# Four of sixteen block transfers issued by ScalarE's queue, and a new order at the end of layer 2

## Chip, cores and metric

The kernel runs on one core of one Trainium2 chip. The metric is device time in microseconds (us), the median of the runs; lower is better.

## The reference

Sixteen independent graphs of 1024 nodes with 64 features pass through four graph-attention layers, each followed by a residual and a layer norm. All four are masked by the same adjacency matrix. Layer 2, at whose loop and end most of the change stands, has eight heads:

```python
def _L2_gnn_ref(atom_embeddings, edges, Wq, bq, Wk, bk, Wv, bv, edge_bias, Wp, bp):
    ...
    scores = jnp.einsum('bmhd,bnhd->bhmn', q, k) * scale
    scores = scores + jnp.transpose(edge_bias[edges], (0, 3, 1, 2))
    scores = jax.nn.leaky_relu(scores, NEG_SLOPE)
    scores = jnp.where(mask, scores, jnp.asarray(-1000000000.0, dtype=scores.dtype))
    attn = jax.nn.softmax(scores, axis=-1)
    out = jnp.einsum('bhmn,bnhd->bmhd', attn, v).reshape(b, m, h * d)
    return out @ Wp + bp
```

Layer 3 scores a pair of nodes by 64 products behind a leaky ReLU:

```python
    s = u[:, :, None, :] + v[:, None, :, :]
    s = jnp.where(s > 0, s, ALPHA * s)
    e = jnp.einsum('bijf,f->bij', s, a[:, 0])
```

## The kernel before, in words

All order is written by hand: each engine has one program, and semaphores tie them together. The programs loop over the graphs. In one turn of the loop an engine does layer 3 of graph g, with layers 0 and 1 of graph g+1 woven into it (`ahead`), and then layer 2 of graph g+1.

**Layer 2** works on 64 tiles of 128 rows by 1024 columns: four pairs of heads, eight row blocks each, two heads. Tiles 2s and 2s+1 are step s (32 steps). One tile passes through:

- TensorE `scores` (L665, L669): mask, then q times x in two parts, into one of two PSUM slots, `score[n % 2]`. It waits until VectorE has read tile n-2 of that slot (`s_leaky`).
- ScalarE `relu` (L944), the first pass, PSUM to `probs[n % 4]`. From tile 4 on it waits until tile n-4 has been turned (`s_blocks`).
- VectorE `leaky` (L1243): adds the score, and finds the least of each row.
- ScalarE `exps` (L951): the exponential, with row sums.
- VectorE `turn_tile`: `dve.transpose` (L1271) turns each 32x32 block within the tile and writes it to `blocks[k % 2]`.

Four tiles (two steps) make a group or quad k. To turn the whole matrix, the 32x32 blocks must still change partitions. That is done by transfers: `move` (L380) on SP's queue issues sixteen, each from 32 partitions to 32 others, 128 KB, into `quadT[k % 3]`. Quads 0 to 14 are moved (`MOVED`). Quad 15 isn't: TensorE turns its four tiles against the identity (L522), and VectorE copies them out of PSUM (L1276) into `blocks[1]`, for which it waits until quad 13 has been moved out of it. VectorE waits for the transfers of quad k-2 before it writes quad k, TensorE for those of quad k before the products.

TensorE `pv_quad` (L697) multiplies the turned quad by the values `vw` in two halves, each 16 matmuls. It is called at step s with quad s//2 - LAG, half s % 2, from s = 2*LAG = 6 on. After the four quads of a pair, ScalarE copies the sums out (`copy_out`, L959, half at t = 2 and half at t = 6 of the next pair), TensorE turns them (`turn_heads`, L522), VectorE divides by the row sums (`pair_out`, L1284), and GpSimd adds. `extra_use` says at which step of a pair q and `vw` of the next pair are made, and heads are turned. For the next graph SP loads eight adjacency tiles between the groups (`next_adj`, L367) and GpSimd converts them out of `adj_in` (L1438 to L1443).

At the end of the program's layer 2 stand the last step, the remaining halves of quads 12 and 13, quads 14 and 15, and the heads of pair 3.

**Start of layer 3**: VectorE adds the last heads (L1364) and normalizes; x2 (L1188) is turned by TensorE. TensorE does first the first products of the next graph (L527, L544) and `KEEP` = 24 matmuls whose result isn't used (L776). From x2 follow v3 and ucol (L1021, L1022 on ScalarE, one half of the partitions each), and with them the 128 groups of the layer: ScalarE (L1035) and VectorE (L1379) make operands, TensorE multiplies (L808). `move` also carries layers 0, 1 (64 KB each) and 3 (32 KB each).

The lines that the change touches most are these:

```python
for turn_ in range(4):
    for a in range(4):
        c = (a + turn_) % 4
        sp.dma_start(dst[32 * c:32 * c + 32, :, a, :], src[32 * a:32 * a + 32, :, c, :]).then_inc(done, 16)
```

## Time and profile before

| | |
|---|---|
| median of 3 runs | 9054.23 us (9046.0 to 9068.25) |
| the profiled execution | 9052.68 us |
| its span, first to last instruction | 9050.9 us |
| mean granted TensorE clock | 0.958 of full speed |
| TensorE, VectorE, ScalarE, GpSimd busy | 90%, 82%, 78%, 16% |
| DMA: the dynamic queue q1 | 810.76 MB, 40.9% of 16 engines' time |

The profile is of one execution. "Busy" is the share of the span in which an engine runs an instruction; issuing transfers doesn't count as busy. "SPq" is the queue of SP. The chain of waits follows the last instruction back to what released it, and so on to the start; its shares tell which engine or queue the end of the program hung on. One graph takes some 553 us: layer 2 about 195, its end and the start of layer 3 some 45, and layer 3 the rest.

### The profile page before, as it was taken

The numbers are of one execution on the slowest core, as the hardware profiler recorded it, in microseconds if no ns is written. First come the engines' busy times: TensorE is split into PE (matmuls) and PEld (weight loads), VectorE is DVE, ScalarE is ACT, GpSimd is POOL, SyncE is SP. The second block draws the span as 40 slices with busy tenths as digits, with TensorE's granted clock in tenths as the row PEclk, the third lists the DMA queues.
The fourth block names the chain that finished last, engine by engine and source line by source line (L and its number), as shares of the span: only waits on it lengthen the run. The fifth ranks groups of instructions, "written<-read, shape, count | busy, mean of one in ns | idle before, by whom it ended". The sixth has DMA issues, their size and how long they took to land.

```text
span 9050.9 us, 165102 instructions
## 1 busy us (share of the span) xinstructions
PE 8158.5 (90%) x57976; PEld 3621.5 (40%) x57976; DVE 7394.6 (82%) x11173; ACT 7034.4 (78%) x8220; POOL 1429.1 (16%) x582
## 2 busy tenths in 40 slices
PE   3899998989999899998998989899898998999999
PEld 1434435343353433434334353443534435343352
DVE  3788787987879878798787978878788787987878
ACT  2788786977869778787787878778688786977877
POOL 0301203021030301203012030120302103021000
PEclk7999999999999999999999999999999999999999
DMA  2715426253362623527145271542715426253251
GB/s 72 159 35 114 101 50 155 42 129 80 66 139 50 144 58 78 129 46 165 37 100 112 47 167 35 114 98 53 155 39 120 91 49 155 44 132 75 56 126 19
DMA packets 2150347, 822.58 MB, mean 91 GB/s; under 512 B 1146914, under 2 KB 2129954, under 8 KB 2147362
## 3 DMA queue, kind: packets, MB, share of 16 engines
q1 hardware_dynamic: 2149410, 810.76, 40.9%
q8 instruction: 507, 8.31, 0.4%
q14 instruction: 430, 3.52, 0.1%
HBM read 76.25 MB, written 4.19 MB: 9 GB/s over the span
## 4 chain that ended last, share of the span: by engine, by line
PE 36%; SPq 21%; DVE 18%; issue 13%; ACT 8%; DMA 3%; DVEq 0%; POOL 0%; ACTq 0%; POOLq 0%
SPq L380 20%; PE psum L808 19%; DVE work L1379 6%; ACT work L1035 5%; PE psum L527 3%; PE psum L697 3%; DVE work L1271 3%; DVE work L1243 3%; PE psum L599 2%; PE psum L522 2%; PE psum L544 1%; PE psum L776 1%; DMA work<-work 1%; PE psum L669 1%; ACT spare L877 1%
## 5 line engine op out<-in xcount | busy, mean ns | idle before, releaser
L808 PE MATMUL psum<-work,pick 128*32 128x512 f32 x32768 | 3758.0, 598 | 198.1 <-DVE work L1379 162.2
L1035 ACT ACTIVATE work<-spare,ucol 128x1024 f32<-128x1024 f32 x3402 | 3633.7, 1147 | 52.0 <-PE psum L808 48.6
L1379 DVE TENSOR_SCALAR work<-spare,ucol 128x1024 f32<-128x1024 f32 x4790 | 3250.2, 745 | 305.8 <-ACT ucol L1022 233.7
L808 PEld LDWEIGHTS psum<-work,pick 128*32 128x32 f32 x32768 | 975.9, 110 | 2532.0 <-issue 2065.5
L944 ACT ACTIVATE work<-psum,beta 128x1024 f32<-128x1024 f32 x1024 | 1138.9, 1112 | 474.0 <-PE psum L669 395.6
L1271 DVE STREAM_TRANSPOSE work<-work 128x1024 f32<-128x1024 f32 x960 | 1191.1, 1241 | 295.3 <-DMA work<-work 177.1
L1243 DVE CUSTOM_DVE_ANT_0 work<-psum,work 128x1024 f32<-128x1024 f32 x1024 | 1225.7, 1197 | 155.0 <-ACT work L944 143.6
L951 ACT ACTIVATE work<-work,least 128x1024 f32<-128x1024 f32 x1024 | 1172.2, 1145 | 54.7 <-DVE least L1243 54.5
L665 PE MATMUL psum<-mask,ident_b 128*128 128x512 bf16 x2048 | 643.5, 397 | 304.3 <-DVE least L1243 301.0
L1460 POOL TENSOR_TENSOR rstd<-rstd,neg_half 128x8 f32<-128x8 f32 x64 | 131.6, 2056 | 4951.5 <-DVE rstd L1182 4951.5
L669 PE MATMUL psum<-x_split,q_hi 128*128 128x512 f32 x2048 | 862.0, 503 | 0.0
L697 PE MATMUL psum<-work,vw 128*64 128x256 f32 x5632 | 701.7, 393 | 0.0
L669 PE MATMUL psum<-x_split,q_lo 128*128 128x512 f32 x2048 | 660.2, 404 | 0.0
L1438 POOL TENSOR_SCALAR mask_next<-adj_in 128x1024 bf16<-128x1024 int32 x120 | 436.4, 3637 | 442.8 <-DMA adj_in<-in_adj 434.7
L697 PEld LDWEIGHTS psum<-work,vw 128*64 128x64 f32 x5632 | 384.4, 140 | 285.6 <-issue 130.2
L669 PEld LDWEIGHTS psum<-x_split,q_hi 128*128 128x128 f32 x2048 | 405.1, 198 | 159.9 <-issue 15.5
L1440 POOL TENSOR_SCALAR no_edge<-adj_in 128x1024 bf16<-128x1024 int32 x120 | 436.1, 3634 | 9.5
L669 PEld LDWEIGHTS psum<-x_split,q_lo 128*128 128x128 f32 x2048 | 398.1, 194 | 92.3
L1146 DVE CUSTOM_DVE_ANT_0 spare<-psum,spare 128x1024 f32<-128x1024 f32 x256 | 311.2, 1216 | 110.5 <-ACT spare L872 107.3
L665 PEld LDWEIGHTS psum<-mask,ident_b 128*128 128x128 bf16 x2048 | 125.2, 99 | 688.3 <-DVE least L1243 524.0
L872 ACT ACTIVATE spare<-psum,sbias 128x1024 f32<-128x1024 f32 x256 | 284.4, 1111 | 91.2 <-PE psum L582 77.9
L599 PE MATMUL psum<-q_lo,vw 128*64 128x256 f32 x2048 | 262.9, 401 | 67.3 <-DMA q_lo<-spare 37.1
(161 smaller groups left out, 6985.1 us busy)
## 6 DMA issues: line engine op xcount, KB each, us to landing
work<-work SPq DMA_DIRECT2D x2560, 128.0 KB, 2.5
spare<-work SPq DMA_DIRECT2D x1280, 128.0 KB, 2.5
adj_in<-in_adj SPq DMA_DIRECT2D x128, 512.0 KB, 4.9
q_lo<-adj_in SPq DMA_DIRECT2D x1024, 64.0 KB, 2.1
q_lo<-spare SPq DMA_DIRECT2D x1024, 64.0 KB, 2.1
work<-work SPq DMA_DIRECT2D x1792, 32.0 KB, 1.9
mask<-mask_next SPq DMA_DIRECT2D x16, 2048.0 KB, 9.3
x_in<-in_x SPq DMA_DIRECT2D x16, 256.0 KB, 9.6
```

What stands on the lines that cost most here:

```text
L380: sp.dma_start(dst[32 * c:32 * c + 32, :, a, :], src[32 * a:32 * a + 32, :, c, :]).then_inc(done, 16)
L599: mm = pe.matmul(dst, values[layer][:, j, :], src[:, j, :, :, :], start=(j < 2), stop=(j >= NT - 2))
L665: pe.matmul(slot[:, cols], ident_b[:], mask[:, t, cols], start=True, stop=False)
L669: mm = pe.matmul(slot[:, cols], left, x_split[:, cols], start=False, stop=(k == 1))
L697: mm = pe.matmul(dst, vw[:, pair % 2, j, F * h:F * h + F], src[:, j, :, h, :].rearrange("p a (t i) -> p a t i", t=2), start=(j == 0), stop ...
L808: mm = pe.matmul(slot[32 * q:32 * q + 32, cols], pick[:, 15 - kk:47 - kk], ring[kk % 4][q][:, cols], start=False, stop=(kk == 15), skip_gr ...
L944: act.activation(probs[n % 4], score[n % 2], ACT.Relu, bias=beta4[:, t, 2 * pair + h:2 * pair + h + 1], scale=GAIN[2]).then_inc(s_relu, 1)
L951: act.activation(probs[n % 4], probs[n % 4], ACT.Exp, bias=least[:, n % 4:n % 4 + 1], scale=-1.0, accum_out=rowsum[:, pair % 2, 2 * t + h: ...
L1035: ins = act.activation(ring[kk % 4][q], v3, ACT.Relu, bias=ucol[:, 4 * T + q, kk:kk + 1])
L1243: dve.tensor_tensor_reduce(probs[n % 4], score[n % 2], probs[n % 4], -ALPHA[2], 3.0e38, ALU.add, ALU.min, least[:, n % 4:n % 4 + 1]).then_ ...
L1271: dve.transpose(dst[:, :, h, half, :], probs[n % 4].rearrange("p (b j) -> p b j", j=32))\
L1379: ins = dve.tensor_scalar(ring[kk % 4][q], v3, ucol[:, 4 * T + q, kk:kk + 1], 0.0, ALU.add, ALU.max)
```

## The change

- SP's `move` gets a number of turns. For a quad of layer 2 it does three (twelve transfers). The fourth (four transfers) is issued by ScalarE in the new `move_quad`, called in its even steps s = 2, 4, ... 30 for quad s//2 - 1, after `relu` of tile 2s+2 and before `exps` of tile 2s+1. It waits for the fourth transpose of the quad, and, as SP does, for the buffers. Both count on the same semaphore.
- `LAG` is 5 and counts steps: `pv_quad` is called from s = 5 on, one step earlier than before. The heads, `vw` and the two `copy_out` of a pair come one step earlier too.
- The unmoved tiles 60 to 63 are copied to `last_rows`: tiles 60 and 61 to `adj_in`, free once GpSimd has converted the next adjacency, and tiles 62 and 63 to `work[4:6]`, free after quad 12. Their products are two halves by row block (`pv_last`), sixteen matmuls of 128 columns each. Step 31 is taken out of the loop and written out.
- The last `pair_out` moves from VectorE's layer 2 to the start of its layer 3, behind the loop's branch. `column_low` goes behind x2. The upper half of ucol is made by VectorE, not ScalarE.
- `KEEP` is 16.

```diff
-LAG = 3
+LAG = 5
-KEEP = 24
+KEEP = 16
...
-            def move(dst, src, done):
-                for turn_ in range(4):
+            def move(dst, src, done, turns=4):
+                for turn_ in range(turns):
...
-                    move(dst, src, s_moved[k % 4])
+                    move(dst, src, s_moved[k % 4], 3)
...
+            def pv_last(it, half):
+
+                in_sbuf(pe, it, ("tile", TILES2 - 3 + 2 * half))
+                src = last_rows[half].rearrange("p (b a h i) -> p b a h i", a=4, h=2, i=32)
+                cols = slice((NT - 2 + half) * P, (NT - 1 + half) * P)
+                for j in range(NT):
+                    for h in range(2):
+                        mm = pe.matmul(outT[F * h:F * h + F, cols], vw[:, (HP - 1) % 2, j, F * h:F * h + F],
+                                       src[:, j, :, h, :], start=(j == 0), stop=(j == NT - 1))
...
-                    if s >= 2 * LAG:
-                        pv_quad(g, it, s // 2 - LAG, s % 2, tail)
+                    if s >= LAG:
+                        pv_quad(g, it, (s - LAG) // 2, (s - LAG) % 2, tail)
...
-                pv_quad(g, it, QUADS - 3, 1, tail)
-                for k in (QUADS - 2, QUADS - 1):
-                    pv_quad(g, it, k, 0, tail)
-                    pv_quad(g, it, k, 1, tail)
+                pv_quad(g, it, MOVED - 2, 0, tail)
+                turn_tile(g, it, TILES2 - 2)
+                pv_quad(g, it, MOVED - 2, 1, tail)
+                turn_tile(g, it, TILES2 - 1)
+                pv_last(it, 0)
+                pv_quad(g, it, MOVED - 1, 0, tail)
+                pv_quad(g, it, MOVED - 1, 1, tail)
+                pv_last(it, 1)
...
+            def move_quad(g, k, tail):
+
+                act.wait_ge(s_blocks, g * 4 * MOVED + 4 * k + 4)
+                if k >= 3:
+                    act.wait_ge(s_pv, g * QUADS + k - 2)
...
+                src = blocks[k % 2].rearrange("p (b c x) -> p b c x", c=4, x=P)
+                dst = quadT[k % 3].rearrange("p (b c x) -> p b c x", c=4, x=P)
+                for a in range(4):
+                    c = (a + 3) % 4
+                    act.dma_start(dst[32 * c:32 * c + 32, :, a, :], src[32 * a:32 * a + 32, :, c, :])\
+                       .then_inc(s_moved[k % 4], 16)
...
                     exps(g, n)
                     if more:
                         relu(g, n + 2)
+                    if s and s % 2 == 0:
+                        move_quad(g, s // 2 - 1, tail)
...
+                if h == 0 and half == 0:
+                    dve.wait_ge(s_mask_next, g + 2)
+                if h == 0 and half == 1:
+                    dve.wait_ge(s_pv, g * QUADS + MOVED - 2)
```

ScalarE's instructions in layer 2 of the first graph, from step 2's first exponential on. Before (L951 is the exponential, L944 the first pass, L899 the copy of a q):

```order
L951 ACTIVATE work,rowsum<-work,least 128x1024 [waits s_leaky]
L944 ACTIVATE work<-psum,beta 128x1024 [waits s_scores,s_blocks]
L951 ACTIVATE work,rowsum<-work,least 128x1024 [waits s_leaky]
L944 ACTIVATE work<-psum,beta 128x1024 [waits s_scores,s_blocks]
L951 ACTIVATE work,rowsum<-work,least 128x1024 [waits s_leaky]
L944 ACTIVATE work<-psum,beta 128x1024 [waits s_scores,s_blocks]
L899 ACTIVATE q_hi<-psum 128x1024 [waits s_turned]
L951 ACTIVATE work,rowsum<-work,least 128x1024 [waits s_leaky]
```

After (the same passes are now L960, L953 and L908):

```order
L960 ACTIVATE work,rowsum<-work,least 128x1024 [waits s_leaky]
L953 ACTIVATE work<-psum,beta 128x1024 [waits s_scores,s_blocks]
L985 DMA work<-work 32x8x128 [waits s_blocks]
L985 DMA work<-work 32x8x128 x3
L960 ACTIVATE work,rowsum<-work,least 128x1024 [waits s_leaky]
L953 ACTIVATE work<-psum,beta 128x1024 [waits s_scores,s_blocks]
L960 ACTIVATE work,rowsum<-work,least 128x1024 [waits s_leaky]
L953 ACTIVATE work<-psum,beta 128x1024 [waits s_scores,s_blocks]
L908 ACTIVATE q_hi<-psum 128x1024 [waits s_turned]
```

The four transfers with their wait now stand between a first pass and the next exponential; this comes fifteen times in a layer.

TensorE's end of layer 2, from the last scores on (L522 turns a tile of `work` or the heads, L697 are products, eight rows to a head and half). Before:

```order
L522 MATMUL psum<-ident,work 128x128 [waits s_probs,s_turn_free]
L522 MATMUL psum<-ident,work 128x128 x7
L522 MATMUL psum<-ident,heads_T 128x128 [waits s_copied,s_turn_free]
L522 MATMUL psum<-ident,heads_T 128x128 x7
L697 MATMUL psum<-work,vw 64x4x2x32 x8
L522 MATMUL psum<-ident,work 128x128 [waits s_probs,s_turn_free]
L522 MATMUL psum<-ident,work 128x128 x7
L697 MATMUL psum<-work,vw 64x4x2x32 [waits s_quad_moved1]
L697 MATMUL psum<-work,vw 64x4x2x32 x7
L522 MATMUL psum<-ident,work 128x128 [waits s_probs,s_turn_free]
L522 MATMUL psum<-ident,work 128x128 x7
L697 MATMUL psum<-work,vw 64x4x2x32 x8
```

After (L523 turns, L695 are products of moved quads, L708 those of the unmoved tiles):

```order
L523 MATMUL psum<-ident,work 128x128 [waits s_probs,s_turn_free]
L523 MATMUL psum<-ident,work 128x128 x7
L695 MATMUL psum<-work,vw 64x4x2x32 [waits s_quad_moved1]
L695 MATMUL psum<-work,vw 64x4x2x32 x7
L523 MATMUL psum<-ident,work 128x128 [waits s_probs,s_turn_free]
L523 MATMUL psum<-ident,work 128x128 x7
L695 MATMUL psum<-work,vw 64x4x2x32 x8
L523 MATMUL psum<-ident,work 128x128 [waits s_probs,s_turn_free]
L523 MATMUL psum<-ident,work 128x128 x7
L708 MATMUL psum<-adj_in,vw 64x128 [waits s_turn_free]
L708 MATMUL psum<-adj_in,vw 64x128 x15
L695 MATMUL psum<-spare,vw 64x4x2x32 [waits s_quad_moved2,s_copied]
```

The turn of pair 2's heads and the second half of quad 12 have gone to an earlier step, and between the last tile's turn and quad 14 stand the products of tiles 60 and 61. Before, quads 14 and 15 followed whole; after, quad 14 and then sixteen L708 for tiles 62 and 63.

## Rows read from the trace of the kernel before

**Rows 1.** The page: busy time by engine, and the chain by line.

```profile
PE 8158.5 (90%) x57976; PEld 3621.5 (40%) x57976; DVE 7394.6 (82%) x11173; ACT 7034.4 (78%) x8220; POOL 1429.1 (16%) x582
...
SPq L380 20%; PE psum L808 19%; DVE work L1379 6%; ACT work L1035 5%; PE psum L527 3%; PE psum L697 3%; DVE work L1271 3%; DVE work L1243 3%; PE psum L599 2%; PE psum L522 2%; PE psum L544 1%; PE psum L776 1%; DMA work<-work 1%; PE psum L669 1%; ACT spare L877 1%
```

**Rows 2.** Timeline of SP's queue, ninth graph: start us, length us, instructions xcount.

```profile
4710.99 11.10 SPq L380 DMA_DIRECT2D spare<-work  x16
...
4722.42 0.36 SPq L367 DMA_DIRECT2D adj_in<-in_adj  x1
...
4759.41 23.14 SPq L380 DMA_DIRECT2D work<-work  x32
```

**Rows 3.** The line L380: duration ns min/median/max.

```profile
L380 SPq DMA_DIRECT2D work<-work x4352: 585/613/2072, 278.9 to 9018.4; - x198
...
L380 SPq DMA_DIRECT2D q_lo<-adj_in x1024: 585/611/1702, 64.5 to 8477.3; - x171
```

**Rows 4.** Timeline of ScalarE, start of layer 2; in brackets: [idle before <-releaser].

```profile
4665.45 1.12 ACT L944 ACTIVATE work<-psum,beta 128x1024 f32<-128x1024 f32 x1
...
4668.10 1.11 ACT L944 ACTIVATE work<-psum,beta 128x1024 f32<-128x1024 f32 x1 [1.53 <-PE psum L669]
...
4674.98 1.12 ACT L944 ACTIVATE work<-psum,beta 128x1024 f32<-128x1024 f32 x1
...
4679.24 1.13 ACT L944 ACTIVATE work<-psum,beta 128x1024 f32<-128x1024 f32 x1
...
4689.51 1.02 ACT L899 ACTIVATE q_hi<-psum 128x1024 fp32r<-128x1024 f32 x1 [4.73 <-PE psum L527]
```

**Rows 5.** ScalarE by line, whole layer 2 (busy, mean ns | idle before); its last exponential.

```profile
L951 ACT ACTIVATE work<-work,least 128x1024 f32<-128x1024 f32 x64 | 73.3, 1145 | 4.3 <-DVE least L1243 4.3
...
L944 ACT ACTIVATE work<-psum,beta 128x1024 f32<-128x1024 f32 x64 | 71.2, 1113 | 29.7 <-PE psum L669 23.5 <-DVE work L1271 6.0
...
L903 ACT ACTIVATE vw<-psum 128x1024 f32<-128x1024 f32 x3 | 3.1, 1027 | 1.6 <-PE psum L564 1.6
...
4859.10 1.15 ACT L951 ACTIVATE work<-work,least 128x1024 f32<-128x1024 f32 x1 [0.87 <-DVE least L1243]
```

**Rows 6.** Timeline of TensorE and VectorE, steps 17 and 18 of layer 2.

```profile
4771.77 1.19 DVE L1243 CUSTOM_DVE_ANT_0 work<-psum,work 128x1024 f32<-128x1024 f32 x1
...
4771.81 0.61 PE L665 MATMUL psum<-mask,ident_b 128*128 128x512 bf16 x2
...
4772.88 1.24 DVE L1271 STREAM_TRANSPOSE work<-work 128x1024 f32<-128x1024 f32 x1
...
4776.51 0.60 PE L665 MATMUL psum<-mask,ident_b 128*128 128x512 bf16 x2
```

**Rows 7.** Timeline of all engines, end of layer 2; then one TensorE group by line.

```profile
4843.64 2.12 POOL L1443 TENSOR_TENSOR mask_next<-mask_next,no_edge 128x1024 bf16<-128x1024 bf16 x1
...
4856.70 1.23 DVE L1276 COPY work<-psum 128x1024 f32<-128x1024 f32 x1 [2.53 <-DMA work<-work]
...
4871.61 3.62 PE L697 MATMUL psum<-spare,vw 128*64 128x256 f32 x32
...
4880.52 1.22 DVE L1284 TENSOR_TENSOR heads_T<-psum,rinv 128x1024 f32<-128x1024 f32 x1 [9.19 <-PE psum L522]
...
L762 PE MATMUL psum<-work,vw 128*64 128x128 f32 x16 | 1.1, 279 | 0.0
```

**Rows 8.** Timeline of all engines, start of layer 3.

```profile
4889.74 0.76 DVE L1188 TENSOR_TENSOR x<-zb,rstd 128x256 f32<-128x256 f32 x2
...
4890.63 6.55 PE L776 MATMUL psum<-mask,ident_b 128*128 128x512 bf16 x24
...
4906.50 0.60 PE L801 MATMUL psum<-mask,ident_b 128*128 128x512 bf16 x2
```

**Rows 9.** Windows: PE, PEld, DVE, ACT, POOL busy; clock, DMA share, GB/s.

```profile
4735.00:4758.00 23.00, 20.87 (x120) 12.30 (x120) 20.63 (x26) 18.64 (x26) 2.46 (x2) 1.00 0.95 212
...
4761.00:4783.00 22.00, 19.40 (x118) 11.42 (x117) 19.93 (x26) 17.62 (x25) 15.06 (x6) 1.00 0.80 181
```

More of the change, by code:

```diff
@@ L64, in extra_use @@
     pair, t = divmod(s, NT)
-    if t == 7 and pair:
+    if t == 6 and pair:
         return ("heads", pair - 1)
     if pair + 1 < HP:
-        return {3: ("q", 2 * pair + 2), 4: ("q", 2 * pair + 3), 6: ("vw", pair + 1)}.get(t)
+        return {3: ("q", 2 * pair + 2), 4: ("q", 2 * pair + 3), 5: ("vw", pair + 1)}.get(t)
     return None
@@ L230, in build @@
         quadT = [quad_of(4), quad_of(16), spare[:]]
-        def turned_quad(k):
-            return quadT[k % 3] if k < MOVED else blocks[k % 2]
+        last_rows = [adj_in[:].rearrange("p a b -> p (a b)").bitcast(F32),
+                     work[:, 4:6, :].rearrange("p a b -> p (a b)")]
         probs3 = [work[:, 6 + i, :] for i in range(2)]
@@ L712, in layer2 @@
                 scores(g, it, 1, tail)
-                for s in range(STEPS2):
-                    pair, t = divmod(s, NT)
+                for s in range(STEPS2 - 1):
                     n = 2 * s
-                    more = s + 1 < STEPS2
                     extra = extra_use(s)
-                    if more:
-                        scores(g, it, n + 2, tail)
+                    scores(g, it, n + 2, tail)
                     if extra:
@@ L985, in layer2 @@
                         elu3(tail)
-                    if t == 2 and pair:
+                    if t == 1 and pair:
                         copy_out(g, pair - 1, 0)
-                    if t == 6 and pair:
+                    if t == 5 and pair:
                         copy_out(g, pair - 1, 1)
@@ L1264, in turn_tile @@
                 k, half, h, moved = in_quad(n)
-                if k >= 2 and half == 0 and h == 0:
+                if moved and k >= 2 and half == 0 and h == 0:
                     dve.wait_ge(s_moved[(k - 2) % 4],
@@ L1283, in pair_out @@
                 filled(dve, it, ("heads", pair))
[L1284 to L1286 removed]
+                pair_times(rinv)
             def layer2(g, it, flagged, tail):
@@ L1315, in layer2 @@
                             final3(tail)
-                pair_out(g, it, HP - 1)
             def either_layer2(g, it, tail):
```

54 lines of the change are left out of this document (33 added, 21 removed).

## Prediction

> **What bounds the kernel now.** I read the page first: TensorE is busy for 90% of the span, VectorE 82%, ScalarE 78%, and the chain that ended last lies on SP's queue for a fifth of the time, all of it in L380, the transfers that turn blocks of probabilities [rows 1]. No engine is full, and a queue that only issues is the second member of the chain, so I looked for the stage in which it is the limit. I follow the ninth graph (layer 2 from 4665.4 us on) and let it stand for all sixteen.
>
> In its layer 2 SP issues 240 transfers for fifteen moved groups of sixteen. From 4710.99 on it has hardly a gap: 11.10 us for one group, an adjacency load, 23.14 us for two, and so to the last [rows 2]. That is 0.69 to 0.72 us for a transfer (11.10/16, 23.14/32). The price is the instruction's, not the bytes': 128 KB and 64 KB transfers have nearly the same median, 0.613 and 0.611 us, though single ones reach 2 us [rows 3]. So a group costs SP 11 to 11.7 us and with the loads some 12. The first ScalarE pass starts at 4665.45 and the last exponential ends at 4859.10+1.15 = 4860.25: 194.8 us for 16 groups, 12.2 each [rows 4, 5]. TensorE needs less: a step with two tiles and half a product goes from 4771.81 to 4776.51, 4.7 us, 9.4 for a group [rows 6]; VectorE needs 1.19 and 1.24 per tile, some 9.5 for a group [rows 6]. SP sets the pace there. But ScalarE is not far: one tile's two passes take (4679.24-4674.98)/2 = 2.13 us [rows 4], 8.5 for a group, and its other passes (six q_hi, three vw, eight half-width ones) add some 12 us to a layer. Its idle time in that layer is 29.7+4.3+4.7+1.6 = 40.3 us [rows 5].
>
> **The change, part by part.** (1) *ScalarE issues four of each group's sixteen transfers.* SP's group falls to 12 x 0.72 = 8.6 us and SP stops being the limit. On ScalarE the four stand between the first pass of tile 4k+6 and the exponential of tile 4k+5, behind a wait for VectorE's transpose of tile 4k+3. In a loop that ScalarE bounds, that transpose ends 1.19+1.24 = 2.4 us after the first pass of tile 4k+5 [rows 6], and ScalarE has by then done an exponential and a pass (2.13): the wait is some 0.25 us, the pass before it is already over, and nothing lies over the issue. What an issue costs on ScalarE, no row shows. Bounds: below, the plain adjacency load, 0.36 us on SP [rows 2], or nothing for what falls beside a running pass; above, the longest L380, 2.07 us [rows 3]. I take SP's dense mean for the same instruction, 0.72. A move then costs 0.25 + 4 x 0.72 = 3.13, fifteen of them 47 us of ScalarE. Of the 40.3 us idle, 1.5 at the second tile and 4.7 before the first q_hi [rows 4] come from the tail of layer 3 and stay: 34 us can be filled. The ledger gives 47-34 = 13 us more than 194.8. The other way, by adding up ScalarE's passes (64 x 2.13 + 12 + 47 + 6.2 + 3 for the waits for q on TensorE), gives 204.6, 10 us more; the difference is the 0.1 us of overlap that each wait now loses. I take the middle, **+11.6 us per graph**. Behind the issuing ScalarE stand the exponential and first pass of tiles 4k+5 and 4k+7, and for them VectorE and then TensorE's score slots, which are two deep: TensorE keeps the waiting that it has today, 12.2-9.4 us per group and a little more, for another engine.
>
> (2) *Order at the end of layer 2.* Today the last exponential ends at 4860.25 and pair_out's L1284 starts at 4880.52: 20.3 us [rows 5, 7]. In between TensorE still does heads, the last half of group 12, both tile turns, group 13, groups 14 and 15 (3.62 each), a copy and a turn; VectorE's copy of a tile had waited 2.53 us for a transfer [rows 7]. In the changed order the products of group 12 and the turn of pair 2's heads are over before tile 63's scores, the unmoved tiles go to rows that wait for no transfer, and behind the last exponential there remain: about 3.1 us of backlog on TensorE (the second half of group 13, held by the turn of tile 62), a turn 1.1, a half of the last products 1.2 (L762's sixteen matmuls of the same 128 columns and 64 rows of output are busy for 1.1 [rows 7]), group 14 3.6, the other half 1.2, the copy 0.65 and the turn 1.1, with 0.4 between them: 12.4 us. **-7.9 us.** Group 14's transfers come 2.4+12x0.72+2.5 = 13.5 us after the first pass of tile 61, TensorE wants them at about 15: covered; with SP's backlog of today they would not be. The wait for the converted mask before tile 60 is over: GpSimd ends it at 4845.76, the copy stands at 4856.70 [rows 7].
>
> (3) *KEEP 24 to 16.* x2 is there by 4889.74+0.76 = 4890.5, yet TensorE runs the 24 filling matmuls from 4890.63 to 4897.18 [rows 8]. So they are on the path. Eight at the mean of 6.55/24 = 0.27 are 2.2; those left out run when the first ones have brought the clock back up, so I take 0.21 each: **-1.7 us**. Only if the clock stays low for longer behind them would it be given back. pair_out moved behind the loop's branch, column_low moved behind x2: both make x2 about 2 us earlier, which the filling matmuls cover: 0. The half of ucol that goes to VectorE frees ScalarE of one short pass, but TensorE has its own work until L801 at 4906.50 [rows 8]: 0. LAG and the uses one step earlier only follow (2).
>
> **Sum.** +11.6 - 7.9 - 1.7 = +2.0 us per graph; sixteen make +32, with up to 10 more because the first and last graphs lack part of the idle time. Against the profiled execution, 9052.7 us (its span is 9050.9; the median of the runs is 9054.2, which is 0.02% off), that is 9085 to 9095: **9090 us, 0.4% slower**. About 0.3% is what a measurement of this kernel can tell from no change.
>
> **Rivals.** *A: ScalarE's issue is dearer.* With transfers of both queues in flight the sixteen DMA engines are busy for 0.95 of a stretch with a load and 0.80 of one without, at 212 and 181 GB/s [rows 9], and SP's long issues are there already. At 1.0 us per issue, half way from the median to the upper part, each graph pays 15 x 4 x 0.28 = 16.8 more: 9360 us. It decides from 0.72 us upward. The Trainium skill, "DMA: Bandwidth & Descriptors", section "Issuing engines are not separate DMA queues", says that all queues share the same DMA engines and that a second issuer saves only sequencer time; its section on queues has the engines alternate between them. With full rings ScalarE's four would then end with SP's first four, eight transfers of 0.62 us (128 KB at 212 GB/s), 4.9 us instead of 2.9, and the time would be 9570. That transfers of half the size cost the same issue time speaks against it.
>
> *B: the other side, faster.* The issue lies beside ScalarE's running pass, or costs it little. If the transpose of tile 4k+3 is done before the pass of 4k+6 starts, which is so wherever TensorE is late (23.5 us of ScalarE's idle time is waiting for its scores [rows 5]), up to 1.0 us of a move is hidden: 15 x 1.0 x 16 = 240 us, 8850. At 0.36 us per issue the loop would save 21 us, but there the DMA engines stop it: 15 x 2.1 MB and 8 x 0.5 MB at 212 GB/s are 168 us of 194.8, and TensorE's own 9.4 us per group leave no more than some 9 us under today's: 16 x (-9-9.6) = -300, 8755. It decides when a move costs ScalarE less than 2.8 us.
>
> *C* is the forecast's own spread: +-4 us per graph in how the idle time is filled, +-64 us.
>
> **Chances.** Forecast (ScalarE takes SP's place as the bound, at SP's price) 0.50, of which slower 0.34, same 0.13, faster 0.03; A 0.20, slower; B 0.30, of which faster 0.28, same 0.02. Together faster 0.31, same 0.15, slower 0.54. The range 8850 to 9340 leaves out the upper half of A (0.10) and the lower third of B (0.10).
>
> **What would show it.** In the changed profile: a second issuing queue with 960 transfers; their mean length (0.72 expected); SP with gaps of 2 to 3 us between groups in layer 2; the chain with ScalarE's queue and first passes where SP's L380 was; 203 to 208 us from first pass to last exponential; 12 to 13 us from there to pair_out; some 1.7 us less filling. I am wrong if layer 2's loop is under 197 us (B) or over 215 (A), or if the end does not shrink.

## The result and the profile after

| | before | changed kernel |
|---|---|---|
| median of the runs | 9061.24 us (9046.0 to 9070.84) | 9556.24 us (9528.23 to 9558.15) |
| ratio, 95% interval | | 1.054 (1.0519 to 1.0562) |
| span of the profiled execution | 9050.9 us | 9552.5 us |
| mean granted TensorE clock | 0.958 | 0.941 |

The kernel got 5.4% slower, 495 us, where 32 to 36 us were forecast. The sign was right. The size lies above the range, where only rival A's mechanism leads.

First the page of the changed kernel: busy time by engine, the chain by line, the two rows in which ScalarE's exponential and first pass stand, and the new queue's transfers.

```profile
PE 8307.6 (87%) x58360; PEld 3716.0 (39%) x58360; DVE 7415.7 (78%) x11189; ACT 6984.4 (73%) x8204; POOL 1431.5 (15%) x582
...
PE psum L817 19%; ACTq L985 8%; ACT work L1063 6%; DVE work L1299 5%; DVE work L1420 4%; PE psum L528 4%; DVE work L1271 4%; PE psum L695 3%; ACT work L953 3%; SPq L381 3%; PE psum L600 3%; PE psum L670 2%; PE psum L523 2%; PE psum L565 1%;
...
L960 ACT ACTIVATE work<-work,least 128x1024 f32<-128x1024 f32 x1024 | 1171.2, 1144 | 788.0 <-issue 696.0
L953 ACT ACTIVATE work<-psum,beta 128x1024 f32<-128x1024 f32 x1024 | 1130.8, 1104 | 159.7 <-PE psum L670 157.8
...
work<-work ACTq DMA_DIRECT2D x640, 128.0 KB, 4.0
spare<-work ACTq DMA_DIRECT2D x320, 128.0 KB, 4.1
```

Every engine is less busy by share than before [rows 1]. SP's queue has fallen from 20% of the chain to 3%, and ScalarE's queue has come in with 8%. The exponential now stands idle for 788 us, 696 of them behind "issue": ScalarE's own sequencer was issuing, and nothing else was late. Before, ScalarE waited for TensorE's scores instead.

One move, from the timeline of all engines in the ninth graph:

```profile
5033.82 1.24 DVE L1299 STREAM_TRANSPOSE work<-work 128x1024 f32<-128x1024 f32 x1
5034.03 1.11 ACT L953 ACTIVATE work<-psum,beta 128x1024 f32<-128x1024 f32 x1
...
5035.09 3.71 ACTq L985 DMA_DIRECT2D work<-work  x4
...
5036.46 1.21 DVE L1271 CUSTOM_DVE_ANT_0 work<-psum,work 128x1024 f32<-128x1024 f32 x1
...
5038.85 1.15 ACT L960 ACTIVATE work<-work,least 128x1024 f32<-128x1024 f32 x1 [3.71 <-DVE work L1299]
...
5041.23 1.23 DVE L1271 CUSTOM_DVE_ANT_0 work<-psum,work 128x1024 f32<-128x1024 f32 x1 [2.39 <-ACT work L953]
...
5042.52 0.61 PE L666 MATMUL psum<-mask,ident_b 128*128 128x512 bf16 x2 [1.37 <-DVE least L1271]
```

The transpose that the issues wait for ends at 5035.06, the pass ends at 5035.14, and the issues run from 5035.09 to 5038.80: the pass covers 0.05 us of them, and nothing the rest. The exponential follows at 5038.85. Then VectorE waits 2.39 us for ScalarE, and TensorE 1.37 us for VectorE. The bracket of the exponential names the transpose, which had long been done: what stood in between were the four issues.

The length of the issues, from the view of the line:

```profile
L985 ACTq DMA_DIRECT2D work<-work x640: 592/817/1755, 278.9 to 9231.6; - x160
L985 ACTq DMA_DIRECT2D spare<-work x320: 592/822/1728, 311.5 to 9244.8; - x160
```

The median is 0.82 us where SP's was 0.61 [rows 3]. By their place in the four they take 0.61, 0.66, 0.94 and 1.42 us (means over all 240 groups), 3.72 us together with the gaps.

ScalarE's idle time by line, layer 2 of the ninth graph (4925.0 to 5155.1; in the kernel before it was 4665.4 to 4860.3):

```profile
L960 ACT ACTIVATE work<-work,least 128x1024 f32<-128x1024 f32 x64 | 73.2, 1144 | 49.2 <-issue 41.7 <-DVE work L1299 7.2 <-DVE least L1271 0.3
L953 ACT ACTIVATE work<-psum,beta 128x1024 f32<-128x1024 f32 x64 | 70.7, 1105 | 8.7 <-PE psum L670 8.4
...
L908 ACT ACTIVATE q_hi<-psum 128x1024 fp32r<-128x1024 f32 x6 | 6.1, 1020 | 19.1 <-issue 13.4 <-PE psum L528 5.7
L912 ACT ACTIVATE vw<-psum 128x1024 f32<-128x1024 f32 x3 | 3.1, 1023 | 1.3 <-PE psum L565 1.3
L1027 ACT ACTIVATE work<-psum,top 128x1024 f32<-128x1024 f32 x1 | 1.1, 1113 | 0.5 <-DVE top L1369 0.5
```

Against [rows 5] the wait for scores has shrunk from 23.5 to 8.4 us. The moves cost 49.2 - 0.3 + 13.4 = 62.3 us (the idle time that ends at an exponential or a q behind an issue), 4.15 each. The rest is 78.8 - 62.3 = 16.5 us. (The idle times at an exponential are those of L960: 41.7 us are put down to issues and 7.2 to the transpose that the issues had waited for.)

TensorE's clock changed too. The profile shows it at one of two levels, 1.2 or 2.4 GHz. At the lower one it stood for 36.7 us of a loop where it was 13.1 us before (means of the sixteen graphs), and TensorE was busy for 182.7 us of a loop instead of 166.9. I cut every layer 2 into fourteen groups, from the first pass of tile 4k+6 to that of tile 4k+10, 224 in all. In 104 of them the clock was low for no more than 1 us; they take 12.95 us, where 177 such groups before took 11.68, and ScalarE never waits for TensorE in them. The other 120 take 16.40 us, where 47 such groups before took 14.11, and all of ScalarE's waiting for TensorE stands in them, 15.0 us per graph. In the ninth graph the clock was low from 5026.5 to 5029.9 and from 5081.1 to 5087.9, and ScalarE's two longest waits for scores, 2.08 and 2.33 us, ended soon after, at 5031.41 and 5090.18. Most of the groups in which q or `vw` is made are among the 120, so the difference is not a price of the clock alone; no run separates the two.

The end of layer 2 and the start of layer 3, from the timeline of all engines:

```profile
5153.93 1.15 ACT L960 ACTIVATE work<-work,least 128x1024 f32<-128x1024 f32 x1 [0.28 <-DVE least L1271]
...
5159.09 1.97 PE L708 MATMUL psum<-adj_in,vw 128*64 128x128 f32 x32
5160.88 3.62 PE L695 MATMUL psum<-spare,vw 128*64 128x256 f32 x32
5164.34 1.92 PE L708 MATMUL psum<-work,vw 128*64 128x128 f32 x32
...
5168.08 1.23 DVE L1312 TENSOR_TENSOR heads_T<-psum,rinv 128x1024 f32<-128x1024 f32 x1 [5.41 <-PE psum L523]
...
5175.00 0.76 DVE L1216 TENSOR_TENSOR x<-zb,rstd 128x256 f32<-128x256 f32 x2 [1.55 <-POOL rstd L1501]
5178.10 6.28 PE L784 MATMUL psum<-mask,ident_b 128*128 128x512 bf16 x16
...
5194.92 3.01 PE L817 MATMUL psum<-work,pick 128*32 128x512 f32 x16 [0.20 <-ACT work L1063]
```

From the last exponential (over at 5155.08) to pair_out's L1312 there are 13.0 us where there were 20.3 [rows 5, 7], in the forecast's order: unmoved half, group 14, unmoved half, copy, turn. The sixteen filling matmuls took 6.28 us here, hardly less than the 24 of before [rows 8]: the granted clock over them was 0.57 in the mean, and 0.81 over those 24.

### The profile page after: what moved, and what is told of

The parts are those of the page before. It is cut to its first block, busy times and chain, and to the rows that moved or that the text cites. A ratio compares the mean times of both kernels' runs of the same rounds, so it can differ in the third digit from the quotient of the medians.

```text
span 9552.5 us, 166201 instructions
## 1 busy us (share of the span) xinstructions
PE 8307.6 (87%) x58360; PEld 3716.0 (39%) x58360; DVE 7415.7 (78%) x11189; ACT 6984.4 (73%) x8204; POOL 1431.5 (15%) x582
## 4 chain that ended last, share of the span: by engine, by line
PE 40%; DVE 18%; issue 15%; ACT 13%; ACTq 8%; SPq 3%; DMA 1%; DVEq 0%; POOL 0%; POOLq 0%
PE psum L817 19%; ACTq L985 8%; ACT work L1063 6%; DVE work L1299 5%; DVE work L1420 4%; PE psum L528 4%; DVE work L1271 4%; PE psum L695 3%; ACT work L953 3%; SPq L381 3%; PE psum L600 3%; PE psum L670 2%; PE psum L523 2%; PE psum L565 1%; PE psum L545 1%
## 5 line engine op out<-in xcount | busy, mean ns | idle before, releaser
L817 PE MATMUL psum<-work,pick 128*32 128x512 f32 x32768 | 3767.1, 599 | 199.2 <-DVE work L1420 167.9
L817 PEld LDWEIGHTS psum<-work,pick 128*32 128x32 f32 x32768 | 979.7, 110 | 2536.4 <-issue 2080.2
L960 ACT ACTIVATE work<-work,least 128x1024 f32<-128x1024 f32 x1024 | 1171.2, 1144 | 788.0 <-issue 696.0
L953 ACT ACTIVATE work<-psum,beta 128x1024 f32<-128x1024 f32 x1024 | 1130.8, 1104 | 159.7 <-PE psum L670 157.8
L666 PE MATMUL psum<-mask,ident_b 128*128 128x512 bf16 x2048 | 667.9, 410 | 517.4 <-DVE least L1271 514.9
L670 PE MATMUL psum<-x_split,q_hi 128*128 128x512 f32 x2048 | 898.5, 522 | 0.0
L670 PE MATMUL psum<-x_split,q_lo 128*128 128x512 f32 x2048 | 682.5, 416 | 0.0
L695 PE MATMUL psum<-work,vw 128*64 128x256 f32 x5120 | 656.8, 401 | 0.0
L695 PEld LDWEIGHTS psum<-work,vw 128*64 128x64 f32 x5120 | 353.4, 142 | 278.9 <-issue 147.8
L908 ACT ACTIVATE q_hi<-psum 128x1024 fp32r<-128x1024 f32 x128 | 130.7, 1021 | 346.2 <-issue 213.0
L528 PE MATMUL psum<-xTa,Aq 65*128 65x512 f32 x512 | 276.5, 666 | 113.4 <-DVE yout L1189 110.0
```

The lines of the kernel that those rows point to most:

```text
L528: mm = pe.matmul(dst[:, c * HALF:(c + 1) * HALF], weights, src[:, c * HALF:(c + 1) * HALF], start=True, stop=True)
L666: pe.matmul(slot[:, cols], ident_b[:], mask[:, t, cols], start=True, stop=False)
L670: mm = pe.matmul(slot[:, cols], left, x_split[:, cols], start=False, stop=(k == 1))
L695: mm = pe.matmul(dst, vw[:, pair % 2, j, F * h:F * h + F], src[:, j, :, h, :].rearrange("p a (t i) -> p a t i", t=2), start=(j == 0), stop ...
L817: mm = pe.matmul(slot[32 * q:32 * q + 32, cols], pick[:, 15 - kk:47 - kk], ring[kk % 4][q][:, cols], start=False, stop=(kk == 15), skip_gr ...
L953: act.activation(probs[n % 4], score[n % 2], ACT.Relu, bias=beta4[:, t, 2 * pair + h:2 * pair + h + 1], scale=GAIN[2]).then_inc(s_relu, 1)
```

## The experiments

All were timed against the kernel before on the same chip. Three lengths will be used for every kernel: the **loop**, from the start of the first first pass of a layer 2 to the end of its last exponential; the **end**, from there to the start of the last pair_out; the **start**, from there to TensorE's first product of layer 3 (L808 of before, L817 of the changed kernel). Each is read in the traces and averaged over the sixteen graphs; the ninth is the one shown in rows. What is left of a graph, from the first product of layer 3 to the next first pass, is 310.6 to 311.6 us in all of them. The last column is the length of ScalarE's block of issues. The medians of before beside which they stand differ by up to 30 us, so a difference between two rows that were timed on different chips is no surer than that.

| kernel | median us | ratio (95% interval) | loop | end | start | ScalarE's block |
|---|---|---|---|---|---|---|
| before | 9061 to 9090 | | 193.1 | 19.5 | 29.0 | |
| changed | 9556 | 1.054 (1.0519 to 1.0562) | 230.7 | 13.0 | 28.3 | 3.72 |
| e1, all on SP | 9015 | 0.9922 (0.9898 to 0.9946) | 195.9 | 15.2 | 27.7 | |
| e2, four on ScalarE alone | 9729 | 1.0718 (1.0695 to 1.0742) | 233.4 | 19.7 | 29.7 | 3.72 |
| e3, e1 and four tiny ones | 9328 | 1.0274 (1.0251 to 1.0296) | 218.3 | 13.8 | 26.2 | 2.86 |
| e4, four spread | 8958 | 0.9872 (0.9846 to 0.9897) | 195.2 | 13.0 | 25.7 | |
| e5, q before the block | 9451 | 1.0409 (1.0381 to 1.0436) | 224.7 | 13.0 | 28.0 | 3.72 |
| e6, a block of two | 9016 | 0.9931 (0.9905 to 0.9957) | 199.8 | 13.0 | 26.7 | 1.3 |
| e7, e1 with KEEP 24 | 9053 | 0.997 (0.9949 to 0.999) | 197.0 | 15.2 | 30.5 | |
| e8, spread later | 8954 | 0.9861 (0.9835 to 0.9888) | 194.7 | 13.0 | 27.4 | |
| e9, two spread | 8961 | 0.9858 (0.9835 to 0.9881) | 195.8 | 13.6 | 26.3 | |
| e10, block of four later | 9410 | 1.0351 (1.0331 to 1.0371) | 223.0 | 13.1 | 27.3 | 3.62 |

**Is it ScalarE's issuing, or the new order?** e1 keeps everything of the change but the share, e2 makes the share alone in the kernel before.

```diff
 e1, against the changed kernel
-                    move(dst, src, s_moved[k % 4], 3)
+                    move(dst, src, s_moved[k % 4])
...
-                    if s and s % 2 == 0:
-                        move_quad(g, s // 2 - 1, tail)
```

> The changed kernel with all sixteen transfers of a moved group issued by SP again; everything else of the change stays. Theory 1 (ScalarE's issuing is what costs): layer 2's loop falls back from 230.7 to about 193 us per graph, the shorter end (13.0 instead of 19.5 us from the last exponential to pair_out) and the 0.7 us of the filling matmuls stay: 16 x (-6.5-0.7) = -115 us against before, about 8940. Theory 2 (the earlier products, heads and vw of LAG = 5 and the new end cost as well): the loop stays above 200, the time above 9060.

> The kernel before, with only one part of the change: ScalarE issues four of the sixteen, in the same place of its order. Theory 1: the loop goes from 193 to about 222 to 231 us, the end stays at 19.5: before + 16 x 30 to 38 = 9540 to 9660 us, as dear as or dearer than the whole change. Theory 2 (half of the loss comes from q, vw and the products standing one step earlier): 9300 to 9400.

e1 is 0.8% faster than before and e2 7.2% slower. Both missed their numbers. e1 lies 75 us above the 8940 of theory 1: its loop is 195.9 us and not 193, and its end 15.2 and not 13.0. e2 lies 69 us above the range of its theory 1. One difference that its trace shows is that ScalarE's copy of `vw` waits behind a block too, 12 us per graph, which it doesn't in the changed kernel. The share of ScalarE costs 541 us in the new order (9556 - 9015) and 646 us in the old one; the new order loses time in neither comparison. All that was lost is in the loop: 34.8 us of 541/16 = 33.8 per graph.

**Is it the issue itself, or the bytes in flight?** e3 leaves all sixteen transfers on SP and has ScalarE issue, at the same place, four more of 2 KB into a tile that nobody reads.

```diff
 e3, against e1
+                for a in range(4):
+                    act.dma_start(small[32 * a:32 * a + 32, :, 0:2], ident[32 * a:32 * a + 32, :].rearrange("p (b x) -> p b x", b=8)[:, :, 0:2])\
+                       .then_inc(s_small, 16)
```

> The kernel of e1, and in the place of the four transfers ScalarE issues four extra ones of the same 32 x 8 pattern that carry 2 KB each from the identity to a spare tile which nobody reads. Theory 1a (an issue costs ScalarE the instruction's 0.6 us and no more when there are no bytes behind it): each 0.61 us, 2.6 us per group, in a loop that SP paces at 12 us: e1 + 100 to 200 us. Theory 1b (the third and fourth issue are slow, 0.94 and 1.42 us, because two queues issue at once, whatever the bytes): the same 3.7 us per group, e1 + 400 us or more. If the issue costs ScalarE nothing: e1 + 0.

The four tiny ones still take 0.61, 0.68, 0.71 and 0.78 us, and the kernel loses 313 us against e1. That lies between the two forecasts: the lengths are near those of theory 1a, and the loss is well above its 100 to 200 us. Theory 1b's "whatever the bytes" is refuted. In its timeline a block is just as bare as in the changed kernel:

```profile
4920.52 1.11 ACT L955 ACTIVATE work<-psum,beta 128x1024 f32<-128x1024 f32 x1
4921.65 2.63 ACTq L977 DMA_DIRECT2D small<-ident  x4
4924.33 1.15 ACT L962 ACTIVATE work<-work,least 128x1024 f32<-128x1024 f32 x1 [2.70 <-DMA small<-ident]
```

And its ledger, ScalarE by line in layer 2 of the ninth graph:

```profile
L962 ACT ACTIVATE work<-work,least 128x1024 f32<-128x1024 f32 x64 | 73.2, 1144 | 39.3 <-DMA small<-ident 29.2 <-DVE work L1292 9.8 <-DVE least L1264 0.3
...
L910 ACT ACTIVATE q_hi<-psum 128x1024 fp32r<-128x1024 f32 x6 | 6.1, 1021 | 17.0 <-DMA small<-ident 7.3 <-PE psum L530 5.7 <-issue 4.0
```

The moves cost 39.3 - 0.3 + 7.3 + 4.0 = 50.3 us in this graph, whose loop is 214.5 us; over all sixteen they cost 48.4 us in the mean, near the 47 of the forecast, and the loop is 218.3 us, not 206.4. So at about the price that was forecast a kernel loses 2.7%, not 0.4%, though SP still issues all sixteen here. With 128 KB behind each, the third and fourth take 0.94 and 1.42 us, and another 228 us are lost (9556 - 9328). SP's own issues grow with them: a mean of 0.80 us in layer 2 of the changed kernel, 0.64 in e1 (adjacency loads counted).

**How much comes back if the block is shorter, or q stands before it?**

```diff
 e6, against the changed kernel: SP issues the other two
-                for a in range(4):
+                for a in range(2):
...
 e5, against the changed kernel
-                    if s and s % 2 == 0:
-                        move_quad(g, s // 2 - 1, tail)
                     if extra and extra[0] == "q":
                         q_high(it, extra[1], s_hi)
                     if extra and extra[0] == "vw":
                         vw_copy(it, extra[1])
+                    if s and s % 2 == 0:
+                        move_quad(g, s // 2 - 1, tail)
```

> The changed kernel with ScalarE issuing two of the sixteen in the same place, and SP fourteen. By the lengths in the changed kernel's trace (0.61, 0.66, 0.94, 1.42 us for the four in turn) a move then costs ScalarE 1.3 us less the last two: 2.4 us x 15 x 16 = 580 us less at most, until SP at 14 x 0.66 = 9.2 us per group or the others bound it: 8980 to 9060. If the cost were a fixed price of touching the queue, or of waiting for the transpose, little of it would go: above 9300.

> The changed kernel, but ScalarE copies q (and vw) before it issues the four transfers of an even step, not after. In the changed kernel q_hi waits 13.4 us per graph behind issues, and TensorE's next products of q and vw wait for it; some 8 us per graph of the loop's growth are waits of this kind beyond the issuing itself. Theory 1 with that share: 5 to 8 us per graph less, 80 to 130 us, about 9430 to 9480. If those waits only change places (ScalarE's issuing is one sum): no change, 9530 to 9570.

Half the block is level with e1: 9015.65 against 9015.48 us, while the runs of each lie 17 and 29 us apart. The timeline of e6:

```profile
4769.12 1.11 ACT L956 ACTIVATE work<-psum,beta 128x1024 f32<-128x1024 f32 x1
4770.18 1.28 ACTq L988 DMA_DIRECT2D work<-work  x2
4771.51 1.16 ACT L963 ACTIVATE work<-work,least 128x1024 f32<-128x1024 f32 x1 [1.27 <-issue]
```

Two issues hold ScalarE for 1.27 us, four for 3.71. Even so the block of two isn't free: the loop is 3.9 us longer than in e1, and only the end, 2.2 shorter, and the start, 1.0 shorter, make up for it. e5 gives back 105 us, 6 us of the loop: a q had to wait up to 4.8 us behind a block, and what VectorE and TensorE do with it came later. That wait I had not priced at all.

**Does an issue lie beside a pass?** e4 issues the same four behind four different passes, e8 the same one pass later, e9 only two of them there, and e10 puts the whole block two passes later.

```diff
 e4, against the changed kernel; move_quad issues transfer a alone
                     exps(g, n)
+                    if s > 2 and s % 2:
+                        move_quad(g, s // 2 - 1, tail, 3)
                     if more:
                         relu(g, n + 2)
                     if s and s % 2 == 0:
-                        move_quad(g, s // 2 - 1, tail)
+                        move_quad(g, s // 2 - 1, tail, 0)
...
                     exps(g, n + 1)
+                    if s and s % 2 == 0:
+                        move_quad(g, s // 2 - 1, tail, 1)
                     if more:
                         relu(g, n + 3)
+                    if s and s % 2 == 0:
+                        move_quad(g, s // 2 - 1, tail, 2)
```

> The changed kernel with ScalarE's four transfers apart: one right behind each of the four passes that follow (first pass of 4k+6, exponential of 4k+5, first pass of 4k+7, exponential of 4k+6). If an issue can lie beside a running pass of 1.0 us, 0.6 us of it is hidden each time, ScalarE pays only the wait for the transpose, and with SP relieved the loop is 185 to 195 us: 8850 to 8960. If each issue holds ScalarE after the pass is over, 60 x 0.65 = 39 us plus the wait stay: loop 205 to 215, 9150 to 9300. If the order q, vw is the cost, it stays near 9450.

> e4 with each of the four transfers one pass later: the first behind the exponential of tile 4k+5, when VectorE's transpose of 4k+3 is long over, so that the wait and the first 0.6 us lie beside a running pass as well (in e4 they were open: some 1.1 us per group). If ScalarE bounds e4: 15 x 1.1 x 16 = 260 us less, 8700. If the transfers' landing bounds it (VectorE's transposes waited 169 us for landings in e4), the later issue gives that back or more: 8950 to 9020.

> ScalarE issues two of the sixteen, one behind the exponential of tile 4k+5 and one behind the first pass of tile 4k+7, and SP fourteen: the spread version with less on ScalarE. Theory (in the spread versions ScalarE's issues cost next to nothing, and the loop is held by the transfers themselves and by TensorE): SP's group is 14 x 0.65 = 9.1 us with two thirds of an adjacency load, below the 12.2 us of a group, so nothing is gained or lost against the spread version of four: 8954 +-30 us. Rival (what bounds the loop at 195 us is still that ScalarE issues, only hidden by halves): two fewer give 15 x 2 x 0.2 us x 16 = 96 us, 8860 us. Rival 2 (SP's fourteen are again too many, as in the version with all sixteen on SP): above 9000 us.

> The changed kernel with ScalarE's four issues still in one block, but two passes later: behind the first pass of tile 4k+7 instead of that of tile 4k+6. The transpose they wait for is then long over. Theory 1 (an issue runs beside passes that are already handed to the engine, so the block pays only what is longer than the passes in front of it): the wait goes and one to two passes of 1.1 us lie beside 3.7 us of issuing, so a group pays 1.5 to 2.6 us instead of 4.15; 15 x 16 x (1.5 to 2.6) = 370 to 620 us less than the changed kernel, about 8950 to 9190 us. Theory 2 (it is the splitting up in the spread version that counts, not the place: a block holds back an exponential and two engines behind it wherever it stands): no more than the wait of 0.4 us is saved, 100 us, 9450 us.

e4 is 1.3% faster than before and 6% faster than the changed kernel, with the same 960 transfers on ScalarE's queue. Its timeline:

```profile
4760.56 1.11 ACT L953 ACTIVATE work<-psum,beta 128x1024 f32<-128x1024 f32 x1
4761.62 0.61 ACTq L985 DMA_DIRECT2D work<-work  x1
4762.27 1.15 ACT L960 ACTIVATE work<-work,least 128x1024 f32<-128x1024 f32 x1 [0.60 <-issue]
4762.31 0.61 ACTq L985 DMA_DIRECT2D work<-work  x1
...
4794.90 1.15 ACT L960 ACTIVATE work<-work,least 128x1024 f32<-128x1024 f32 x1 [1.44 <-PE psum L695]
4794.94 1.71 ACTq L985 DMA_DIRECT2D work<-work  x2
...
4796.05 1.10 ACT L953 ACTIVATE work<-psum,beta 128x1024 f32<-128x1024 f32 x1
4796.74 1.37 ACTq L985 DMA_DIRECT2D work<-work  x1
4797.04 1.14 ACT L960 ACTIVATE work<-work,least 128x1024 f32<-128x1024 f32 x1
```

The first issue, behind the wait for the transpose, still costs the exponential 0.60 us. The second starts at 4762.31, 0.04 us after the exponential has started at 4762.27, and is over before that pass is. The one at 4796.74 took 1.37 us, twice the usual, and lay wholly beside two passes. So a long issue costs nothing as long as passes stand ahead of it in the engine; a block costs what is left of it when they have run out.

e8 and e9 tell how far this goes. e8 hides the first issue too, e9 has half as many, and both give what e4 gives (8954, 8961, 8958). e9's expectation holds: with the issues spread, the time is the same for two and for four of them, and for fourteen and for twelve on SP.

e10 missed its expected range of 8950 to 9190 us and came near the rival's: 9410, 147 us less than the changed kernel. Its timeline and its ledger of the ninth graph show why:

```profile
5029.99 1.12 ACT L953 ACTIVATE work<-psum,beta 128x1024 f32<-128x1024 f32 x1 [2.57 <-PE psum L670]
5030.07 3.62 ACTq L985 DMA_DIRECT2D spare<-work  x4
5033.74 1.15 ACT L960 ACTIVATE work<-work,least 128x1024 f32<-128x1024 f32 x1 [2.63 <-DVE work L1299]
```

```profile
L960 ACT ACTIVATE work<-work,least 128x1024 f32<-128x1024 f32 x64 | 73.3, 1146 | 39.6 <-DVE work L1299 28.2 <-DVE least L1271 6.1 <-issue 5.3
L953 ACT ACTIVATE work<-psum,beta 128x1024 f32<-128x1024 f32 x64 | 70.9, 1107 | 26.7 <-PE psum L670 26.6
```

The block starts 0.08 us into the pass and 1.1 us of it is covered, as theory 1 had it: the idle time behind it is 2.63 us instead of 3.71. But the wait comes back at another place. ScalarE now waits 26.6 us in a layer for TensorE's scores where the changed kernel waited 8.4. TensorE has two score slots, and around a block it stops: in this graph it stood idle for 2.29 us before the scores at 5023.46 and for 2.75 us before those at 5037.41, both times for VectorE, which had waited for ScalarE's first pass. Part of the late scores is the clock: it was at 1.2 GHz from 5024.7 to 5028.1, and half a product took 3.46 us there where others take 1.95. Groups of this graph that ran at 2.4 GHz wait 0.9 to 1.3 us before the pass that hides the block, those with a low stretch mostly 1.2 to 2.6, once 3.9. The step that failed in theory 1 is that it let ScalarE use at once every microsecond that the cover saves.

**Is KEEP worth its forecast?**

```diff
 e7, against e1
-KEEP = 16
+KEEP = 24
```

> The kernel of e1 (all sixteen on SP) with KEEP back at 24. The prediction's term: eight filling matmuls fewer give 1.7 us per graph, so this is 27 us (0.3%) slower than e1, 9040 beside 9015. The rival: what they save is given back by a lower clock in the products behind them (from pair_out to the first ring product only 0.7 us was gained between before and changed kernel): e1 + 0 to 12 us.

The timelines of the ninth graph, first of e7 and then of e1 (one record is missing in each stretch):

```profile
4908.83 7.26 PE L784 MATMUL psum<-mask,ident_b 128*128 128x512 bf16 x23 [0.33 <-issue]
```

```profile
4889.29 5.81 PE L784 MATMUL psum<-mask,ident_b 128*128 128x512 bf16 x15 [0.33 <-issue]
```

Eight fewer take 1.45 us less in this pair, the start is 2.8 us shorter in the mean, and the medians are 37 us apart where 27 were forecast. The runs of e1 lie within 30 us of each other and those of e7 within 68, and their intervals against before just miss each other (0.9898 to 0.9946 and 0.9949 to 0.999). The 2.8 us of the start are a weak witness: the execution of e7 that was profiled took 30 us more than its median, and kernels that all have KEEP 16 show starts of 25.7 to 28.3 us. So sign and order of size are supported, the exact size is not.

## Why the prediction was right or wrong

**The mechanism of part 1 held, its sum did not.** ScalarE took SP's place, the issues stand behind the wait for the transpose with no pass over them, and TensorE waits for another engine. But part 1 was forecast at +11.6 us per graph, and the loop grew by 230.7 - 193.1 = 37.6. Two terms failed.

**The first: the price of a move was a quarter too small.** The step "I take SP's dense mean for the same instruction, 0.72" failed: it is 0.93 us per issue with its gap, 3.72 for four. The wait was forecast at 0.25 us and is 4.15 - 3.72 = 0.43. The moves cost 62.3 us, not 47; that is 15.3 us per graph, or 245 of the 466 us by which the time lies above the forecast. SP's dense mean already contained contention, but contention got worse with two queues issuing 128 KB each at once: 1.42 us for the fourth. Rival A put in 1.0 us and got 9360 us: its price was 8% too high, and its time 196 us too low. So the price is about half of the error and not the whole.

**The second: how idle time was set off against it.** The step is "34 us can be filled. The ledger gives 47-34 = 13 us", and with it "I take the middle, +11.6". With 62.3 us of moves and a growth of 37.6, 24.7 were filled. In e3, with 48.4 us of moves and a loop 25.2 us longer than before, 23.2 were. So about 24 us can be filled, whether the moves cost 48 or 62 us, and 10 of the 34 were not there to fill. That accounts for the rest of the error in the loop: 15.3 + 34 - 24.7, and 1.4 for the middle that I took instead of the ledger's 13, make the 26.0 us between 11.6 and 37.6. Both figures come from the ledger by what ended each wait; they say how much was left, not why.

The ninth graph tells where it stands. In the changed kernel 16.5 us of idle time other than the moves remain, where I had 9.2 in the ledger that gave 204.6 us and 6.2 in the one that gave 13 us more than 194.8. The ninth loop is 230.1 us. From 204.6 one gets there by 15.3 for the price, 7.3 for the other waits and 2.9 for passes that I had rounded down (busy and overlapping time of ScalarE 230.1 - 78.8 = 151.3 us, where 64 x 2.13 + 12 = 148.3 stood in the sum).

Why about 24 and not 34 stays open. Two things are seen. ScalarE, VectorE and TensorE are tied by two score slots, so idle time at one tile need not be there for a stop at another; no run had another number of slots. And groups that ran at 2.4 GHz took up most of their moves: 12.95 us with a move of some 4 us in them, where they took 11.68 before. I had put the clock in the loop at nothing without a reason; but the low stretches grew from 13.1 to 36.7 us and all of ScalarE's waits for TensorE stand in groups that have one. In e3 they were 27.1 us, and in the spread versions e4, e8 and e9 14 to 15. Whether the low clock held the loop up or only followed from TensorE's stops, no run separates.

**"SP sets the pace there" was wrong too, though the loss covered it.** I set a group's 12.2 us against 9.4 of TensorE, read from a step in which only two tiles and half a product were done. The windows of the middle of layer 2 (tiles 16 to 60, eleven groups), in this order for before, e1, e4, e9 and the changed kernel, say otherwise; columns as in [rows 9]:

```profile
4715.61:4846.32 130.71, 119.22 (x690) 70.58 (x686) 108.39 (x141) 105.92 (x145) 66.94 (x24) 1.00 0.89 200
```

```profile
4718.47:4848.95 130.48, 117.53 (x679) 71.07 (x688) 108.34 (x141) 105.48 (x145) 64.12 (x24) 1.00 0.90 204
```

```profile
4673.32:4799.49 126.17, 116.23 (x669) 70.19 (x678) 108.48 (x141) 105.03 (x144) 63.54 (x23) 1.00 0.98 211
```

```profile
4678.18:4809.00 130.82, 118.81 (x679) 71.50 (x688) 109.08 (x141) 104.61 (x145) 64.12 (x24) 0.99 0.93 206
```

```profile
4984.49:5140.43 155.94, 127.88 (x680) 75.05 (x680) 109.56 (x141) 103.82 (x146) 63.30 (x23) 0.93 0.72 170
```

TensorE is busy for 119.22/11 = 10.8 us of each group's 11.9, and the DMA engines for 0.89 of the stretch. SP's relief could win 1 us per group at most; in e9, with SP at fourteen and hardly anything paid on ScalarE, the middle takes as long as in e1. In e4 it is 4 us shorter in this graph, with the DMA engines at 0.98, but the mean of the loops is the same. Whether TensorE or the DMA engines hold these loops at some 195 us no run separates. In the changed kernel's middle the granted clock was 0.93, and TensorE was busy for 127.88 us with the same work. The chain had SP's queue at 20% before, at 22% in e1 and at 10% in e4, and the loop is 193, 196 and 195 us: the share of a chain is no price for what stands in it. This agrees with the section that the prediction named, "Issuing engines are not separate DMA queues" of the Trainium skill's "DMA: Bandwidth & Descriptors": a second issuer saves only sequencer time. In the loop that was worth nothing (195.8 us in e9, 195.9 in e1). At the end it was worth something: TensorE waits 1.97 us for the transfers of group 14 in e1's ninth graph and not at all in e4's or the changed kernel's, and the end is 13.0 us instead of 15.2, some 35 us of the whole time. The time of 9570 us that the prediction worked out from its alternating engines lies 14 us from the result, and that is luck: four issues took 3.72 us, not 4.9, and the rest came from idle time that was not filled.

**Part 2 held.** The end was forecast at -7.9 us and measured at 19.5 to 13.0, -6.5 (20.3 to 13.0 in the ninth graph, from which the forecast was made). That group 14's transfers would not be covered with SP's backlog of before was right too, as e1 shows. **Part 3** held in e1 against e7. In the changed kernel itself the start lost only 0.7 us, and the filling matmuls took 6.28 us in the ninth graph. The clock was low there from 5169.8 to 5183.5, so over nearly all of them; before, it was low from 4882.9 to 4893.1 and high for the larger part of the 24. That is the prediction's own exception ("Only if the clock stays low for longer behind them"). **"LAG and the uses one step earlier only follow (2)"** is not quite right: the loop of e1 is 2.8 us longer than before's. No run separates LAG from the uses, so this stays open.

**Rival B** had the right mechanism for another kernel. A pass has to run when the issue comes, which isn't so in the changed kernel, is so for the last three issues in e4, and for every one in e8 and e9. Its forecast of 8755 to 8850 us wasn't reached there either: the loop is at most 1.2 us shorter than e1's, and the 58 us between e4 and e1 are almost all in the end and the start.

**The measures named.** Second queue with 960 transfers: yes. Mean of 0.72: 0.91. Gaps of 2 to 3 us in SP's queue: the twelve transfers took SP 9.9 to 11.7 us a group in the middle of the ninth graph and not 8.6, with gaps of 3.6 and 6.9 us at some groups and none at others. The chain: SP's transfers fell from 20% to 3%, and ScalarE's queue (8%) and first pass (3%) came in. Loop of 203 to 208: 230.7, over the 215 that were to speak for A. 12 to 13 us at the end: 13.0. 1.7 us less filling: 0.3 in the ninth graph.

**The best version** measured is e8, 8954 us, 0.9861 (0.9835 to 0.9888) of before; e4 and e9 are no different from it.

## What to carry to other kernels

Before a transfer is given to an engine that also computes, look at what stands ahead of it in that engine's program. Directly behind a wait its whole issue time is lost to the engine; behind a pass that is already running it is free up to the length of the passes that stand ahead of it. So give such an engine its issues one at a time between passes. Four in one block lost 5.4% here, two in one block cost 3.9 us of the loop, and four spread out cost nothing that could be measured. And idle time summed over a stage is only an upper bound on what can be filled: of the 34 us that looked free here, about 24 were. Look also at what a stop does to TensorE's clock, which a sum of waits doesn't contain.

## What was not expected of the hardware

- For the first two issues of a block the time hardly depends on the bytes: 0.61 and 0.68 us for 2 KB, 0.61 and 0.66 for 128 KB. For the third and fourth it does: 0.71 and 0.78 us for 2 KB beside SP's sixteen large ones (e3), 0.94 and 1.42 us for 128 KB beside SP's twelve, and SP's own mean rose from 0.64 to 0.80. What in the path of the descriptors makes the third one slow, no run separates.
- Spread out, the same four have a median of 0.61 us in e4, but a mean of 0.75: the fourth still takes 1.04. In e9 the two have a median of 0.59 and a mean of 0.60.
- The engine's pass and its sequencer's issue run side by side. An issue need not wait for the pass ahead of it in the program to start. In 224 groups of e4 (the first fourteen of each layer), the second issue starts 0.04 us after that pass has started in 176 and up to 0.85 us before it in the other 48. The third and the fourth start before it in 191 and 200 of them, up to 1.27 us earlier, while the pass before that one is still running: the one at 4796.74 began 0.30 us before the exponential ahead of it (4797.04). None of the three ever starts more than 0.04 us after the start of the pass ahead of it.
- The transfers land later when two queues issue: 4.0 us after ScalarE's issues, and 3.0 after SP's where all on SP took 2.4.
